# A state-space stage computed channels first, with its sum of squares made on TensorE

## The chip, the cores and the metric

The kernel runs on one core of a Trainium2 chip. The metric is the device time of one execution in microseconds. The kernel before has a median of 1835.91 us over three runs (1831.64 to 1842.42); the execution that was profiled took 1837.23 us, and the profile's span, from its first instruction to its last, is 1835.4 us. A measurement of this kernel tells a change of about 0.5% from none.

## The reference, cut to what matters

The program is two transformer-like layers. Its first part, the one that is changed, is a state-space mixer on 2 sequences of 512 tokens and 512 features, 64 heads of 64 channels in 8 groups of 8 heads:

```python
proj = hidden @ in_proj.T                    # gate 4096, x 4096, B 1024, C 1024, dt 64
xBC  = silu(conv_bias + causal 4-tap convolution of (x, B, C))
dt   = softplus(dt + dt_bias);  dA = exp(-dt * exp(A_log))
state = state * dA[t] + (dt[t] * x[t]) outer B[t]        # per head, 64 x 128
y[t]  = state @ C[t] + D * x[t]
yn    = y * rsqrt(mean(y*y over the group's 512 channels) + 1e-5) * norm_weight
out  += (yn * silu(gate)) @ out_proj.T
```

Behind it come a gated feed-forward layer with ternary weights, attention with 32 heads of 16 channels, and a layer of 8 experts of which each token takes 2, with norms and residual sums between them. They are the same in both kernels.

## The kernel before, in words

Every engine has a program of its own, written out by hand, and the engines meet only in semaphores; the order of each queue is the order of the code. The state-space stage is `step(g, s, first, last)` in each of the four engines' blocks. `group_steps` calls it for group 0 unrolled, groups 1 to 6 in a hardware loop, and group 7 unrolled with two more steps to drain. A step `s` is one tile of 128 tokens (`NT` = 8 tiles, `CH` = 4 per sequence), and it is a software pipeline: tile `s` is transposed and its decay matrices are made, tile `s-1` gets its outputs `y`, tile `s-2` is normalised and multiplied with the output projection. Steps 0, 1, 2, 4, 5 and 6 also make two of the 12 convolution tiles (6 per sequence, 128 channels by 512 tokens) for later steps; steps 3 and 7 make none (`conv_tiles`). In group 7 the steps from 4 on make none.

Products that need more than one pass are split in a high and a low half in `fp32r` (`products`, L344: 12 products of 128 by 128 by 512 for each 512 x 512 result tile). `low` (L349) makes the low half by a subtraction. Other products are plain fp32, and each of them is two records on TensorE.

In one step of the kernel before:

- TensorE: four transposes of `xbc` into bank 4 (L1482), B's transpose and the product of B and C (L1486, L1488), the sums of decays from `am` (L1496), the first convolution tile, four transposes of `yn` of tile `s-2` into bank 4 (L1515), `yo` = C times the state in bank 6 (L1523, 128x512, only where a state has entered, that is in 6 of 8 steps), `yi` in bank 7 as eight products, one for each head, `em` stationary and 64 columns of `dtx` moving (L1529), the new state's product in bank 6 (L1538, waits until VectorE has read `yo`), the second convolution tile, the gate product of tile `s` in bank 0, and the output product of tile `s-2` in bank 1. Tokens are on the partitions in `yo`, `yi`, `y`, gate and `yn`.
- VectorE: `btok` and `gmask` (L1170, L1173), `em` times `gmask` (L1176, waits for ScalarE's exponential), `y` = bank 6 times the growth `cur` (L1186), the three taps of the first convolution (L1100), `ynTl` (L349), `y` plus bank 7 (L1199), `y` plus `xd` (L1202; L1206 where no state entered), the state (L1212, L1215), `silu` (L1106), the second tile's taps, the gate `sg` (L1225), `yn` = `y` times `rg` times `sg` (L1233), `silu`, and the accumulation in `acc` (L1240). In step 3 it also subtracts two of the next group's `wcl`. In group 7 `norm_round` for the next layer follows L1240.
- ScalarE: the copy of `xtok` out of bank 4 (L881), the exponential `em` (L889), the first tap and the tanh of each convolution tile (L856, L864), `ynTh` out of bank 4 (L900), the square of `y` with its sum in `ss` (L907), the gate's tanh (L913). In step 3 it casts the next group's `wch`, at the end of step 7 the gate's (`gate_high`, L923) and scales the output weights (L926), in step 2 it casts those.
- GpSimd: the decays `am` of the next tile (L640, two of 128x1024), the state's decay (L667), `dtx`, `xdec` and `xd` = D times x (L677, L682, L686), the root `rg` (L691, L694), the low halves `wol` in step 2, `wcl` (two) in step 3 and `wgl` in step 7.
- SP: for each group the loads of `w_conv` (once `wgl` and `wol` are done), then `w_gate` and `w_out` (once `wcl` is done), all into the buffer `x`: gates in rows 0 to 3, outputs in 4 to 7.

Before the loop the first sequence's six convolution tiles of group 0 are made, with ScalarE and VectorE finishing each one before bank 0 or 2 is free again. In group 7 SP reloads the residual `hidden` into `x`.

Of the kernel before, what the change touches and what calls it, by code (L numbers as in the profile page):

```python
# [14 lines left out]
P = 128  # L15
# [42 lines left out]
def program(nc, hidden, w_conv, w_gate, w_dt, conv_w, conv_b, dt_bias, A_log, Dskip, norm_w, w_out,  # L58
            ff_gu, ff_dn, gate_s, up_s, down_s, wq, wk, bqk, wv, bv, wo, bo, gate_w, expert_w, out):
    ctx = ExitStack()  # L60
    with ctx:
# [55 lines left out]
        per = sa("per", [P, 5 * NT + 1, H])  # L117
        cur = sa("cur", [P, 5 * NT + 1, HG])
# [14 lines left out]
        xd = sa("xd", [P, GI])  # L133
        bcast = xd[:, 0:2 * H].rearrange("p (a h) -> p a h", a=2)
        state = sa("state", [P, GI])
        y = sa("y", [P, GI])
        ss = sa("ss", [P, 2])
        ssv = sa("ssv", [P, 2])
        rg = sa("rg", [P, 2])
        yn = sa("yn", [P, GI])  # L140
        sg = sa("sg", [P, 2, GI])
        ynTh = sa("ynTh", [P, GI], F32R)
        ynTl = sa("ynTl", [P, GI], F32R)
# [129 lines left out]
        am_ready, xd_ready, xdec_ready, dtx_ready, sdec_ready = (sem(s) for s in ("am_ready", "xd_ready", "xdec_ready", "dtx_ready", "sdec_ready"))  # L273
        m_ready, yo_ready, yo_used, yi_ready, y_part, y_ready = (sem(s) for s in ("m_ready", "yo_ready", "yo_used", "yi_ready", "y_part", "y_ready"))
        st_ready, state_ready, ss_ready, ssv_ready, rg_ready = (sem(s) for s in ("st_ready", "state_ready", "ss_ready", "ssv_ready", "rg_ready"))
        gate_ready, tg_ready, gate_used, yn_ready, yn_tr, o_ready, out_added = (sem(s) for s in ("gate_ready", "tg_ready", "gate_used", "yn_ready", "yn_tr", "o_ready", "out_added"))
# [58 lines left out]
        gate_stage, out_stage = x[:, 0:KT, :], x[:, KT:2 * KT, :]  # L335
# [31 lines left out]
        CONV_BANKS = (0, 2)  # L367

# [71 lines left out]
        def _(sp):  # L440
# [5 lines left out]
            sp.dma_start(per[:, 5 * NT, :], Dskip.partition_broadcast(P)).then_inc(small_in, 16)  # L446
# [6 lines left out]
            sp.dma_start(gate_stage, w_gate[0]).then_inc(wg_in, 16)  # L453
            sp.dma_start(out_stage, w_out[0]).then_inc(wo_in, 16)
            with sp.Fori(0, G - 1) as g:

                sp.wait_ge(wg_lo, KT * g + KT)
                sp.wait_ge(wo_lo, KT * g + KT)
                sp.dma_start(conv_stage(1), w_conv[bass.ds(g + 1, 1)]).then_inc(wc_in, 16)

                sp.wait_ge(wc_lo, 2 * g + KT + 2)
                sp.wait_ge(wc_lo2, 2 * g + KT + 2)
                sp.dma_start(gate_stage, w_gate[bass.ds(g + 1, 1)]).then_inc(wg_in, 16)
                sp.dma_start(out_stage, w_out[bass.ds(g + 1, 1)]).then_inc(wo_in, 16)
            sp.wait_ge(wg_lo, KT * G)
            sp.wait_ge(wo_lo, KT * G)
            for i in range(NT):
                sp.dma_start(x[:, i, :], hidden[i * P:(i + 1) * P, :]).then_inc(x_in, 16)
# [153 lines left out]
        def _(pool):  # L622
# [28 lines left out]
            def step(g, s, first, last):  # L651
                if s < NT and not (last and s == NT - 1):
# [11 lines left out]
                if s >= 1 and 1 <= c < CH - 1:  # L664

                    pool.wait_ge(yo_ready, entered(g, i) + c)
                    pool.tensor_tensor(pair(state[:, :]), pair(state[:, :]), heads(4 * NT + i),  # L667
# [3 lines left out]
                if s < NT:  # L671

                    pool.wait_ge(x_out, NT * g + s + 1)
                    src = pair(xtok[:, s % 2, :])
                    if not (first and s == 0):
                        pool.wait_ge(yi_ready, NT * g + s)
                    pool.tensor_tensor(pair(dtx[:, :]), src, heads(NT + s), ALU.mult).then_inc(dtx_ready, 1)  # L677
                    if s % CH < CH - 1:
# [3 lines left out]
                        pool.tensor_tensor(pair(xdec[:, :]), src, heads(3 * NT + s), ALU.mult).then_inc(xdec_ready, 1)  # L682
                if s < NT:
                    if not (first and s == 0):
                        pool.wait_ge(y_ready, NT * g + s)
                    pool.tensor_tensor(pair(xd[:, :]), src, heads(5 * NT), ALU.mult).then_inc(xd_ready, 1)  # L686
                if not (first and s == 0) and s <= NT:

                    n = NT * g + s
                    pool.wait_ge(ss_ready, n)  # L690
# [10 lines left out]
                if s == NT - 1 and not last:  # L701
                    gate_low(g + 1)
# [1163 lines left out]
```

## Time and profile before

| | |
|---|---|
| median of three runs | 1835.91 us |
| the profiled execution | 1837.23 us, span 1835.4 us |
| TensorE, products | 1620.2 us busy, 88% of the span |
| VectorE | 1297.8 us, 71% |
| GpSimd | 1006.7 us, 55% |
| ScalarE | 755.8 us, 41% |
| granted TensorE clock, mean | 0.940 of full |
| chain that ended last | TensorE 66%, VectorE 13%, GpSimd 7% |
| `yi` products (L1529) | 1024 records, mean 272 ns, 121.3 us |
| DMA | 79.7 MB, 43 GB/s |

A busy share is the time in which an engine worked on an instruction, over the whole span. Records of TensorE overlap: one that lasts 0.39 us can be followed by the next after 0.23 us, so starts are compared with starts. In the profile's rows PE is TensorE's products, PEld its weight loads, DVE VectorE, ACT ScalarE, POOL GpSimd. PEclk is the granted clock, 1.00 for 2.4 GHz and 0.50 for 1.2 GHz.

### The profile page before, as it was taken

The numbers are of one execution on the slowest core, as the hardware profiler recorded it, in microseconds if no ns is written. First come the engines' busy times: TensorE is split into PE (matmuls) and PEld (weight loads), VectorE is DVE, ScalarE is ACT, GpSimd is POOL, SyncE is SP. The second block draws the span as 40 slices with busy tenths as digits, with TensorE's granted clock in tenths as the row PEclk, the third lists the DMA queues.
The fourth block names the chain that finished last, engine by engine and source line by source line (L and its number), as shares of the span: only waits on it lengthen the run. The fifth ranks groups of instructions, "written<-read, shape, count | busy, mean of one in ns | idle before, by whom it ended". The sixth has DMA issues, their size and how long they took to land.

```text
span 1835.4 us, 25172 instructions
## 1 busy us (share of the span) xinstructions
PE 1620.2 (88%) x8696; PEld 1272.0 (69%) x8696; DVE 1297.8 (71%) x2037; ACT 755.8 (41%) x1389; POOL 1006.7 (55%) x861
## 2 busy tenths in 40 slices
PE   3699989999999999999999877997489999988692
PEld 2478768777877787778777656886356676767581
DVE  5687888787888778787778856555636776768525
ACT  2443433434434434434343213333136766664231
POOL 3376775776767767757766835003433443328554
PEclk9899999999999999999999978999589999998696
DMA  4001020020010010200201001212000000032344
GB/s 134 1 35 47 1 79 3 0 80 0 34 46 0 34 46 0 80 0 0 80 0 43 38 1 64 69 69 92 0 0 13 1 13 1 1 147 83 100 142 160
DMA packets 23303, 79.73 MB, mean 43 GB/s; under 512 B 6464, under 2 KB 6592, under 8 KB 17984
## 3 DMA queue, kind: packets, MB, share of 16 engines
q1 hardware_dynamic: 19552, 66.73, 10.1%
q0 software_dynamic: 3680, 12.06, 2.0%
q8 instruction: 43, 0.70, 0.2%
q14 instruction: 28, 0.23, 0.0%
HBM read 68.56 MB, written 10.22 MB: 43 GB/s over the span
## 4 chain that ended last, share of the span: by engine, by line
PE 66%; DVE 13%; POOL 7%; issue 6%; ACT 4%; DMA 3%; SPq 1%; POOLq 0%; DVEq 0%; ACTq 0%
PE banks L344 35%; PE banks L1597 6%; PE banks L1529 3%; PE banks L1716 3%; PE banks L1607 2%; PE banks L1538 2%; PE banks L1496 2%; DMA x<-in_w_conv 2%; PE banks L1675 2%; POOL wol L349 2%; PE banks L1706 2%; DVE acc L558 2%; POOL am L640 1%; DVE nmax L1322 1%; DVE tap L1100 1%
## 5 line engine op out<-in xcount | busy, mean ns | idle before, releaser
L640 POOL TENSOR_TENSOR am<-ah,upto 128x1024 fp32r<-128x1024 f32 x64 | 129.3, 2021 | 217.9 <-PE banks L1496 203.6
L1100 DVE SCALAR_TENSOR_TENSOR tap<-banks,parg,tap 128x511 f32<-128x511 f32 (+2 forms) x288 | 214.9, 746 | 30.3 <-ACT tap L856 23.5
L1176 DVE TENSOR_TENSOR em<-em,gmask 128x1024 f32<-128x1024 f32 x64 | 129.3, 2020 | 91.4 <-ACT em L889 90.9
L791 POOL TENSOR_SCALAR kz<-kst,head 128x512 fp32r<-128x512 f32 x64 | 99.1, 1568 | 160.0 <-DVE kst L1306 160.0
L344 PE MATMUL banks<-xTh,wch 128*128 128x512 f32 x384 | 166.4, 433 | 3.7 <-POOL wcl L349 2.4
L640 POOL TENSOR_TENSOR am<-al,upto 128x1024 fp32r<-128x1024 f32 x64 | 160.7, 2511 | 0.0
L344 PE MATMUL banks<-xTh,wcl 128*128 128x512 f32 x384 | 151.7, 395 | 0.0
L344 PE MATMUL banks<-xTl,wch 128*128 128x512 f32 x384 | 151.4, 394 | 0.0
L1032 ACT ACTIVATE prob<-banks,nmax 128x128 f32<-128x128 f32 (+3 forms) x256 | 121.8, 530 | 54.5 <-DVE nmax L1322 54.3
L1529 PEld LDWEIGHTS banks<-dtx,em 128*128 128x128 f32 x1024 | 123.2, 192 | 23.0 <-issue 21.3
L1322 DVE TENSOR_REDUCE nmax<-banks 128x2 f32<-128x256 f32 (+3 forms) x128 | 104.7, 818 | 40.4 <-PE banks L1707 40.3
L856 ACT ACTIVATE tap<-banks,parg 128x512 f32<-128x512 f32 x96 | 74.7, 778 | 139.7 <-PE banks L344 132.0
L864 ACT ACTIVATE th<-tap 128x512 f32<-128x512 f32 x96 | 60.5, 630 | 149.0 <-DVE tap L1100 146.1
L1529 PE MATMUL banks<-dtx,em 128*128 128x64 f32 x1024 | 121.3, 272 | 0.0
L344 PE MATMUL banks<-wgh,xTh 128*128 128x512 f32 x256 | 116.4, 455 | 0.8 <-DVE tap L1100 0.8
L344 PE MATMUL banks<-woh,ynTh 128*128 128x512 f32 x256 | 103.4, 404 | 5.8 <-DVE ynTl L349 5.8
L344 PE MATMUL banks<-wgl,xTh 128*128 128x512 f32 x256 | 105.5, 412 | 0.0
L1716 PE MATMUL banks<-ident,prob 128*128 128x128 f32 x640 | 95.6, 276 | 10.7 <-DVE pB L1332 7.2
L344 PE MATMUL banks<-wgh,xTl 128*128 128x512 f32 x256 | 105.0, 410 | 0.0
L344 PE MATMUL banks<-wol,ynTh 128*128 128x512 f32 x256 | 103.0, 402 | 0.0
L344 PE MATMUL banks<-woh,ynTl 128*128 128x512 f32 x256 | 102.6, 401 | 0.0
L349 POOL TENSOR_TENSOR awl<-prob,awh 128x512 fp32r<-128x512 f32 x8 | 10.1, 1298 | 160.5 <-ACT awh L988 131.5
(289 smaller groups left out, 4471.3 us busy)
## 6 DMA issues: line engine op xcount, KB each, us to landing
x<-in_w_conv SPq DMA_DIRECT2D x7, 1536.0 KB, 6.6
x<-in_w_gate SPq DMA_DIRECT2D x8, 1024.0 KB, 4.8
x<-in_w_out SPq DMA_DIRECT2D x8, 1024.0 KB, 6.8
eraw<-in_expert_w SPq DMA_DIRECT2D x8, 1024.0 KB, 7.2
gur<-in_ff_gu SPq DMA_DIRECT2D x7, 1024.0 KB, 4.8
x<-in_hidden SPq DMA_DIRECT2D x16, 256.0 KB, 4.3
mates<-yd SPq DMA_DIRECT2D x8, 512.0 KB, 4.3
dnr<-in_ff_dn SPq DMA_DIRECT2D x7, 512.0 KB, 3.5
```

The lines of the kernel that those rows point to most:

```text
L344: m = nc.tensor.matmul(o, a, b, start=first and n == 0, stop=last and n == len(terms) - 1)
L640: m = pool.tensor_tensor(am[:, part, :, :], a[:, i, :].bitcast(F32).unsqueeze(2).to_broadcast([P, HG, P]), upto[:, :].unsqueeze(1).to_broa ...
L791: m = pool.tensor_scalar(kz[:, quad % 2, p2, j, :], kst[:, p2, :].bitcast(F32), head[:, j:j + 1], None, ALU.mult)
L856: nc.scalar.activation(tap[:, q % 2, :], bk(CONV_BANKS[q % 2]), ACT.Identity, bias=parg[:, CT * KC + q:CT * KC + q + 1], scale=parg[:, KC ...
L864: nc.scalar.activation(th[:, :], tap[:, q % 2, :], ACT.Tanh).then_inc(tanh_ready, 1)
L1032: e = nc.scalar.activation(prob[:, n % 2, j, 0:kw], bk(2 * (n % 2) + j)[:, 0:kw], ACT.Exp, bias=nmax[:, n % 2, j:j + 1])
L1100: nc.vector.scalar_tensor_tensor(tap[:, q % 2, sh:L], bk(CONV_BANKS[q % 2])[:, 0:L - sh], parg[:, KC * q + k:KC * q + k + 1], tap[:, q % 2 ...
L1176: nc.vector.tensor_tensor(em[:, s % 2, :, :], em[:, s % 2, :, :], gmask[:, :].unsqueeze(1).to_broadcast([P, HG, P]), ALU.mult).then_inc(m_ ...
L1322: nc.vector.tensor_reduce(nmax[:, n % 2, :], banks[:, 2 * (n % 2):2 * (n % 2) + 2, 0:kw], AX, ALU.max, negate=True).then_inc(max_ready, 1)
L1529: m = mat(bk(7)[:, h * HP:(h + 1) * HP], em[:, i % 2, h, :], dtx[:, h * HP:(h + 1) * HP], start=True, stop=True)
L1597: m = mat(bk(2 * w + ft), gu[:, k, ft, w, :], part[:, k, tok], start=(k == 0 and part is xTh), stop=(k == KT - 1 and part is xTl))
L1716: m = pe.transpose(bk(4 + j)[:, c * P:(c + 1) * P], prob[:, w % 2, j, c * P:(c + 1) * P], ident[:, :])
```

## The change

The stage is turned: `y`, `yn` and the gate have channels on the partitions and tokens in the free dimension, so that `yn` needs no transpose before the output product.

- `yi`: `dtx` (64 columns) is stationary, `em` (128 columns) moves; the even heads' outputs go to partitions 0 to 63, the odd ones' to 64 to 127. `yo`: four products with 128 columns of the state stationary and C moving.
- The growth factors now run along the free dimension. They are made once for all heads, stored in DRAM (`grownT`), and for each tile where a state has entered SP loads them broadcast, by two DMAs into the single buffer `grown`, a row of `x`.
- `D * x` is no longer a GpSimd product: `skipped` adds it with four `scalar_tensor_tensor` on 128 columns each, reading `xbc`.
- The norm's factor is now a per-partition scalar only after the output product, so `rg` moves into the accumulation in `acc`. `y` is multiplied with the gate in place. The sum of squares: ScalarE squares `y` into `ysq`, four products of `ysq` with a column of ones add it up in bank 4, ScalarE scales it and adds eps (`ssv`), GpSimd takes the root.
- The four transposes of `yn` and `xd` go. `ynTh` and `ynTl` read `y` in SBUF.
- The gate is made in tiles of 128 channels by 512 tokens, three before the loop and one in each step; the last group has none in steps 5 to 7. The casts and low halves of the gate's weights move from step 7 to step 5, the load of `w_out` behind them.
- VectorE does `ynTl` ahead of the `em` multiply, and in steps without convolution tiles the entered part of `y` too.

```diff
-                    for j in range(KT):
-                        m = pe.transpose(bk(4)[:, j * P:(j + 1) * P], yn[:, j * P:(j + 1) * P], ident[:, :])
-                    m.then_inc(yn_tr, 1)
+                    for j in range(KT):
+                        m = mat(bk(4)[:, 0:1], ysq[:, j, :], ones[:, 0:1], start=(j == 0), stop=(j == KT - 1))
+                    m.then_inc(ss_ps, 1)
...
-                        mat(bk(6), xbc[:, JC, tok], state[:, :], start=True, stop=True).then_inc(yo_ready, 1)
+                        for j in range(KT):
+                            m = mat(bk(6)[:, j * P:(j + 1) * P], state[:, j * P:(j + 1) * P], xbc[:, JC, tok], start=True, stop=True)
+                        m.then_inc(yo_ready, 1)
...
                     for h in range(HG):
-                        m = mat(bk(7)[:, h * HP:(h + 1) * HP], em[:, i % 2, h, :], dtx[:, h * HP:(h + 1) * HP],
-                                start=True, stop=True)
+                        m = mat(bk(7)[h % 2 * HP:h % 2 * HP + HP, h // 2 * P:(h // 2 + 1) * P], dtx[:, h * HP:(h + 1) * HP],
+                                em[:, i % 2, h, :], start=True, stop=True)
...
+                def entered_part():
+                    at_least(dve, ynT_lo, NT * g + i)
+                    if c > 0:
+                        dve.wait_ge(yo_ready, m + c)
+                        dve.wait_ge(grown_in, 32 * (m + c))
+                        nc.vector.tensor_tensor(y[:, :, :], kt(bk(6)), grown, ALU.mult).then_inc(yo_used, 1)
+
+                def skipped(base):
+                    for k in range(KT):
+                        n = nc.vector.scalar_tensor_tensor(y[:, k, :], xbc[:, k, i % NT * P:(i % NT + 1) * P], skipg[:, k:k + 1],
+                                                           base[:, k, :], ALU.mult, ALU.add)
+                    n.then_inc(y_ready, 1)
...
+                if not (first and s < 2):
+                    dve.wait_ge(ynT_hi, NT * g + s - 1)
+                    low(nc.vector, ynTl[:, :, :], y[:, :, :], ynTh[:, :, :]).then_inc(ynT_lo, 1)
+                if s < NT:
+                    if s > 0 and not tiles:
+                        entered_part()
                     dve.wait_ge(e_ready, NT * g + s + 1)
...
+                if making:
+                    dve.wait_ge(sq_ready, NT * g + i + 1)
+                    dve.wait_ge(gate_used, NT * g + 4 + KT * (i // CH) if i >= 0 else NT * g)
+                    nc.vector.tensor_tensor(y[:, :, :], y[:, :, :], gate_at(i % NT), ALU.mult).then_inc(yn_ready, 1)
...
-                    nc.vector.tensor_tensor(acc[:, i % NT, :], acc[:, i % NT, :], bk(1), ALU.add).then_inc(out_added, 1)
+                    dve.wait_ge(rg_ready, NT * g + i + 1)
+                    nc.vector.scalar_tensor_tensor(acc[:, i % NT, :], bk(1), rg[:, i % 2:i % 2 + 1], acc[:, i % NT, :],
+                                                   ALU.mult, ALU.add).then_inc(out_added, 1)
...
+            def grown_load(g, i):
+                at_least(sp, yo_used, entered(g, i) + i % CH - 1)
+                for u in range(2):
+                    sp.dma_start(grown[HP * u:HP * u + HP, :, :],
+                                 halves[u][bass.ds(g, 1), :, i * P:(i + 1) * P].rearrange("g k t -> (g k) t").partition_broadcast(HP)
+                                 ).then_inc(grown_in, 16)
```

## Rows read from the trace of the kernel before

**Rows 1.** Stretches: the first and the last of the seven groups, busy by engine, clock

```profile
core 0: us, PE busy (x) PEld busy (x) DVE busy (x) ACT busy (x) POOL busy (x), PEclk, DMA share, GB/s
81.30:201.40 120.10, 114.94 (x558) 92.18 (x559) 96.28 (x129) 51.31 (x87) 87.99 (x68) 0.97 0.09 31
...
832.40:958.60 126.20, 122.71 (x609) 98.76 (x608) 99.64 (x139) 52.49 (x89) 87.64 (x69) 0.97 0.08 29
```

**Rows 2.** Stretches: steps 0, 2, 3 and 7 of group 3, and its sum

```profile
454.80:470.70 15.90, 15.90 (x83) 13.05 (x82) 13.33 (x21) 8.59 (x15) 13.04 (x10) 1.00 0.00 0
...
486.60:503.40 16.80, 16.80 (x84) 13.46 (x83) 12.92 (x17) 7.58 (x13) 14.82 (x11) 1.00 0.23 83
503.40:519.00 15.60, 12.97 (x60) 10.14 (x59) 12.85 (x17) 6.86 (x11) 13.34 (x10) 0.89 0.03 12
...
567.60:579.90 12.30, 11.44 (x60) 9.00 (x59) 9.24 (x14) 5.34 (x10) 10.16 (x9) 1.00 0.00 0
sum 125.10, PE 121.61 PEld 98.22 DVE 100.10 ACT 52.41 POOL 87.65; mean PE 15.20 PEld 12.28 DVE 12.51 ACT 6.55 POOL 10.96
```

**Rows 3.** Waits of TensorE over the whole span: total us, times, longest

```profile
PE banks L1538 <- DVE y L1186: 32.6, 18, 5.5
...
PE banks L1482 <- DVE xbc L1106: 6.8, 1, 6.8
```

**Rows 4.** Timeline of step 3 of group 3: start, us, engine, line

```profile
505.13 0.60 PE L1515 MATMUL banks<-ident,yn 128*128 128x128 f32 x4
505.56 1.02 PE L1523 MATMUL banks<-state,xbc 128*128 128x512 f32 x2
...
505.91 0.28 DVE L1170 COPY btok<-banks 128x128 f32<-128x128 f32 x1
...
506.42 1.89 PE L1529 MATMUL banks<-dtx,em 128*128 128x64 f32 x16
...
507.52 2.68 DVE L1176 TENSOR_TENSOR em<-em,gmask 128x1024 f32<-128x1024 f32 x1 [1.13 <-ACT em L889]
...
510.95 1.10 PE L1538 MATMUL banks<-xdec,btok 128*128 128x512 f32 x2 [2.63 <-DVE y L1186]
...
512.87 1.04 POOL L686 TENSOR_TENSOR xd<-xtok,cur 128x512 f32<-128x512 f32 x1 [0.77 <-DVE y L1202]
...
513.87 0.91 POOL L691 TENSOR_TENSOR ssv<-ss,epsc 128x1 f32<-128x1 f32 x1
...
515.98 3.69 POOL L349 TENSOR_TENSOR wcl<-x,wch 128x768 fp32r<-128x768 f32 x2
```

**Rows 5.** Timeline of TensorE at the router, products with few columns

```profile
1670.12 0.40 PE L344 MATMUL banks<-awl,attTh 128*128 128x512 f32 x1
1670.35 0.39 PE L344 MATMUL banks<-awh,attTl 128*128 128x512 f32 x1
1670.59 0.95 PE L1756 MATMUL banks<-rw,yb 128*128 128x8 f32 x8
1671.43 0.33 PE L1765 MATMUL banks<-ident,acc 128*128 128x128 f32 x1
```

**Rows 6.** Attention, products on 32-column tiles: timeline, then its weight loads (min/median/max ns)

```profile
1444.25 0.82 PE L1716 MATMUL banks<-ident,prob 128*128 128x128 f32 x6
1445.01 0.86 PE L1675 MATMUL banks<-pA,v 128*32 128x256 f32 x16
1445.79 0.50 PE L344 MATMUL banks<-xTh,aqh 128*128 128x512 f32 x1
...
L1675 PEld LDWEIGHTS banks<-pA,v x16: 106/110/110, 1445.0 to 1445.5; 128*32 128x32 f32 x16
```

**Rows 7.** Lines L1186 and L1202 on VectorE: min/median/max ns, first and last start

```profile
L1186 DVE TENSOR_TENSOR y<-banks,cur x48: 675/679/694, 114.9 to 1083.3; 128x512 f32<-128x512 f32 x48
...
L1202 DVE TENSOR_TENSOR y<-y,xd x48: 691/948/4382, 119.1 to 1085.3; 128x512 f32<-128x512 f32 x48
```

**Rows 8.** DMA issues: a load broadcast to all partitions, KB, us to landing

```profile
dsb<-in_down_s SPq DMA_DIRECT2D x1, 256.0 KB, 3.4
```

**Rows 9.** Stretch: step 6 of the last group

```profile
1046.50:1065.60 19.10, 13.59 (x60) 10.28 (x59) 13.93 (x20) 3.41 (x6) 13.63 (x15) 0.82 0.00 0
```

More of the change, by code:

```diff
@@ L651, in step @@
             def step(g, s, first, last):
+                if s == 5 and not last:
+                    gate_low(g + 1)
                 if s < NT and not (last and s == NT - 1):
@@ L868, in step @@
                 tiles = conv_tiles(s, last)
+                gate = gate_of(s, last)
+                i = s - 2
                 if s == 4 and tiles:
@@ L941, in _ @@
             tanh(0, 0)
-            for n, row in enumerate((2, 3, 4)):
+            for n, row in enumerate((2, 3)):
                 act.wait_ge(dt_cum, n + 1)
@@ L1150, in _ @@
                 silu(q, q, 0)
+                if q >= 3:
+                    gate_made(q - 2, (1, 7)[(q - 3) % 2], 0, q - 3)
             dve.wait_ge(consts, 7)
@@ L1155, in step @@
                 tiles = conv_tiles(s, last)
+                gate = gate_of(s, last)
+                i, c = s - 1, (s - 1) % CH
+                m = entered(g, i)
+                making = not (first and s == 0) and s <= NT
+                def entered_part():
[9 more added lines that the diff above has]
+                    n.then_inc(y_ready, 1)
                 if s == 4 and not last:
@@ L1472, in step @@
                 tiles = conv_tiles(s, last)
+                gate = gate_of(s, last)
                 if s < NT:
@@ L1541, in step @@
                     convolved(n0 + tiles[1], tiles[1] % CT, tiles[1] // CT % NB)
-                if s < NT:
-                    if s == 0:
-                        pe.wait_ge(wg_lo, KT * g + KT)
+                if gate:
+                    if s == 5:
+                        pe.wait_ge(wg_lo, KT * g + 2 * KT)
                     if tiles:
                         pe.wait_ge(taps, 3 * (n0 + tiles[0]) + 3)
-                    elif not (first and s == 0):
-                        pe.wait_ge(gate_used, NT * g + s)
-                    tok = slice(s * P, (s + 1) * P)
-                    products(bk(0), [(xTh[:, k, tok], xTl[:, k, tok], wgh[:, k, :], wgl[:, k, :])
-                                     for k in range(KT)]).then_inc(gate_ready, 1)
+                    else:
+                        pe.wait_ge(gate_used, NT * g + s + 3)
+                    gated(*gate, 0)
                 i = s - 2
```

252 lines of the change are left out of this document (153 added, 99 removed).

## The prediction, made before the changed kernel was run

> **What bounds the kernel now.** I read the page's busy shares first (they stand in the table above). They are means over four stages, so next come the stretches by head group [rows 1]. Seven groups of the state-space stage take 81.3 to 958.6 us, 48% of the span, and the eighth follows. Then one group by its eight steps [rows 2]: TensorE busy 121.6 of 125.1 us, VectorE 100.1. Where a step has convolution tiles, TensorE is busy for all of it (15.90 of 15.90, 16.80 of 16.80): only its own work counts there. Step 3 has no tiles and no such cover: 15.6 us, busy 12.97, granted clock 0.89. Step 7 loses about 1 us. The list of waits says which [rows 3]: the state product (L1538) waited 32.6 us for `y` (L1186). The timeline of step 3 [rows 4] shows it: the products with `em` end near 508.2, the state product starts at 510.95, and a part of the step behind this pause runs at the lower of the clock's two levels, which is how its mean comes to 0.89. L1186 waits because VectorE takes the `em` multiply first (507.52, 2.68 us).
>
> What should a whole group cost TensorE? Step 3's own work is a 16.8 us step without two tiles of 12 products, 0.233 us apart (two of this kind start at 1670.12 and 1670.35 [rows 5]), 11.2 us; likewise step 7. So 4 x 15.9 + 2 x 16.8 + 2 x 11.2 = 119.6 us. Seven groups would be 837.2, less 5.6 in group 0, whose first two steps have no output product: 831.6. They take 877.3 (81.3 to 958.6) [rows 1]. **45.7 us are stall or low clock**; the rest is bound by content.
>
> **Part 1, TensorE's content.** All of it is on the path in a full step.
> - Out: four transposes of `yn`, 0.43 us (505.13 to 505.56 [rows 4]). In: four fp32 products of `ysq` with one column. An fp32 product is two records, as L1523 x2 shows. The nearest row is the router's fp32 product with an 8-column moving side and a 128-column load: eight records in 0.84 us, 1670.59 to 1671.43 [rows 5]; fewer columns can't make it cheaper, as a record there advances at 0.108 us while 8 columns stream for almost nothing, so the load is the price. Bounds 0.43 to 0.95, taken 0.84: **+0.41**.
> - `yo`: one product of 512 columns (0.86 us, 505.56 to 506.42 [rows 4]) becomes four of 128, eight records at 0.11: **+0.03**, in 6 of 8 steps.
> - `yi`: now 16 records of 128-column loads and 64 columns; a record alone lasts 0.27 (table), so (1.89 - 0.27)/15 = 0.108 us each, 1.73 us together [rows 4]. The load sets that pace. Turned, loads are 64 columns and 128 columns stream, and the products alternate between the two column halves of the array. Twice the columns in the same number of records: everything hangs on the halves running together. The nearest row is the attention's product with `v` [rows 6]: 16 records on 32-column tiles, eight of 256 and eight of 128 columns, take 0.78 us to the next line; in a row they would be 8 x 0.21 + 8 x 0.108 = 2.6 us. So four tiles do overlap, loads included. Its edges cost: six transposes from 1444.25 on, 0.11 apart, so the last starts at 1444.80, and the first tiled record at 1445.01, 0.21 where 0.11 is usual, and on leaving the same, 0.1 each way. So 8 x 0.108 + 0.2 = 1.06 us: **-0.67**. Bounds: 0.86 (no edges) to 1.93 (halves in turn).
>
> Sum: -0.26 a step, +0.03 in six of eight: in 56 steps -14.6 + 1.3 = **-13.3 us**.
>
> **Part 2, the wait of step 3 and 7.** Steps without tiles now do `ynTl` and then `y` = `bk(6)` x `grown` ahead of the `em` multiply. In step 3 `yo` is through 1.9 + 0.84 + 0.89 = 3.6 us after its start, `y` at 4.4 to 4.6, and TensorE is ready for the state product at 4.7. The wait goes, and with it the low clock behind it. What is late next: the weights of the next group. TensorE reaches them 11.2 + 1.5 = 12.7 us after the step's start; GpSimd's last `wcl` ends at 516.0 + 3.7 = 519.7 now [rows 4], 16.3 after. It loses `xd` (1.04), the wait for `y_ready` ahead of it (0.77) and `ssv` (0.91); that puts it at 13.6, some 1 us late. VectorE and GpSimd then subtract at once and stretch each other, so I leave 1.5 us a group. Recovered: 45.7 - 7 x 1.5 = **-35.2 us**.
>
> **Part 3, VectorE, ScalarE, GpSimd.** `y + xd` becomes four instructions on 128 columns: `btok` on 128 columns takes 0.28 [rows 4], so 1.1 us for the 0.69 of one L1202 (bounds 0.7 and, should two SBUF inputs meet GpSimd as L1202's do at the median, 1.5). `ynTl` moves ahead of `em`, into time in which VectorE waits for the exponential; it now reads SBUF twice. The rows show what that means: the L1186 with one PSUM input never passes 0.694 us, L1202 with two SBUF inputs has median 0.948 and maximum 4.38 [rows 7]. VectorE is busy 12.5 us of a mean 15.6 [rows 2], so +0.4 us lies under TensorE: counted zero; without that cover it is 64 x 0.4 = 26 us. The square loses its accumulator read and gains a 128x1 activation; GpSimd is relieved. The gate casts and lows move from step 7 to step 5, in front of `em` and the decays: four casts put the exponential some 2 us later, and four subtractions of 1.3 us end near 7.5 us of the step, while the product that needs them starts near 10 (behind both convolution tiles). Hidden.
>
> **Part 4, DMAs.** 96 loads of 128 KB, two for each of six `grown`, one buffer. The nearest is a 256 KB broadcast, 3.4 us to landing [rows 8]. From one `y` to the next lie 10 us or more, so it is hidden, also on SP's queue: the load for step 4 stands behind `w_conv`, the loads for 7 and 0 behind `w_out`, each with a step to spare. If not hidden: up to 3.4 us in 48 steps.
>
> **Part 5, both ends.** Three gate products move ahead of the loop. There VectorE sets the pace and TensorE's first transposes (L1482) wait 6.8 us for its last one [rows 3]; but the last convolution now stands behind two gates (2 x 2.8), which wait for `wgl`. Estimated **+5.7** (3 to 9). In the last group steps 5 to 7 have no gate. Step 6 (19.1 us) runs at a mean clock of 0.82 [rows 9] and is a chain through `y`, state product, gate product, `sg` and output; the twelve gate products fall out of it, between 2.8 us at full clock and 5.6 at half, and `y` no longer stands behind `em` (2 us): -4.4; step 7 -3.7; steps 3, 8 and 9 about -1.3, -1.3 and -0.9; steps 0 to 2, 4 and 5 -1.5 together: **-13** (5 to 18).
>
> **Sum.** -13.3 - 35.2 - 13 + 5.7 = -55.8. The profiled execution took 1837.2 (span 1835.4 and 1.8 around it), 0.1% over the median 1835.9: **1781.5 us**, some 3%.
>
> **Rivals.**
> - *The stall stays.* `grown` or the weights arrive late in step 3 (DMA, or GpSimd and VectorE stretching one another). For: [rows 7], and only one `grown` buffer. Against: 10 us from one use to the next. -35 falls away: 1817.
> - *The halves run in turn*, loads hidden: `yi` 1.93 us. Against: [rows 6]. 64 x 0.87 more: 1837, no change.
> - *Slower: the halves run in turn and each load stands open.* Load records of 32 columns last 0.11 us [rows 6]; 16 x (0.108 + 0.11) + 0.2 = 3.7 us for `yi`, 64 x 2.6 more: 1951. It decides from `yi` above 1.93. Against it speak [rows 6]: there 16 loads and 16 products share 0.78 us. The Trainium skill ("TensorE: Matmul & The Clock Gate", Part 3, Packing small matmuls) says that a weight load overlaps matmuls in flight only where the row group differs; here all products use all rows, and by that rule this rival would be the outcome. The trace does not agree: in [rows 6], with all rows in use too, the loads are hidden.
> - *The change does nothing for TensorE's order*: excluded, 13 us are content.
>
> The skill's "TensorEngine Tiling (Array Packing)", Key Properties, has the array drain when the tiling mode changes; [rows 6] agree, with 0.1 us at each edge.
>
> **Numbers.** Forecast 0.75, its own range 1755 to 1808: `yi` 0.86 to 1.3 (-13, +15), 0 to 3 us left in a group (-10, +10), the ends (-8, +11), not all at once. Stall stays 0.13; in turn 0.07; slower 0.05. A measurement tells about 0.5% (9 us) from no change: faster 0.88, same 0.07, slower 0.05. The range reaches to the stalled case: 1755 to 1820.
>
> **What would show it.** Right: `yi`, 16 records with 128x128 moving, about 1.1 us to the next line; the `ysq` records 0.84; loop groups of 119 to 120 us; step 3 at 11 to 13 us with clock 1.00 and nothing waited for on `y` by the state product. Wrong: `yi` of 1.7 us or more; a wait of `y` on the `grown` DMA; VectorE busy through whole steps with TensorE waiting for taps or `gate_used`; loop groups still near 125.

## The result and the profile after

The changed kernel takes **1841.05 us** (median of 20 runs, 1839.62 to 1843.11) against 1834.72 us (20 runs, 1831.29 to 1844.32) of the kernel before: a ratio of **1.0033**, 95% interval 1.0023 to 1.0043. By the bound of 0.5% that is no change, though the interval puts it some 0.3% on the slow side; it is 59.6 us above the forecast. The profiled span is 1839.2 us where it was 1835.4.

The page shows TensorE a little less busy than before, VectorE 78 us busier, GpSimd 69 us less busy, and VectorE's share of the chain up from 13% to 21%:

```profile
PE 1605.8 (87%) x9254; PEld 1270.5 (69%) x9254; DVE 1375.8 (75%) x2223; ACT 759.5 (41%) x1390; POOL 938.1 (51%) x733
...
PE 67%; DVE 21%; issue 5%; ACT 3%; POOL 3%; DMA 1%; SPq 0%; DVEq 0%; POOLq 0%; ACTq 0%
...
x<-grownT SPq DMA_DIRECT2D x96, 128.0 KB, 4.8
```

The stretches show where. These are steps 0 to 4 and 7 of group 3 and their sum of eight, then the last of the seven groups and the sum of seven (us, then busy by engine, granted clock, DMA share, GB/s); they answer to [rows 1, 2]:

```profile
468.50:484.25 15.75, 15.75 (x92) 13.15 (x91) 14.09 (x23) 8.36 (x14) 6.93 (x5) 1.00 0.07 17
484.25:499.83 15.58, 15.58 (x86) 12.69 (x85) 15.31 (x23) 6.22 (x10) 7.31 (x5) 1.00 0.00 0
499.83:517.00 17.17, 16.63 (x95) 13.59 (x93) 14.96 (x19) 7.58 (x13) 14.38 (x10) 1.00 0.31 93
517.00:529.70 12.70, 11.60 (x70) 9.07 (x69) 12.37 (x18) 6.75 (x11) 10.40 (x7) 1.00 0.19 40
529.70:551.73 22.03, 17.58 (x92) 14.32 (x91) 18.22 (x26) 6.23 (x10) 9.80 (x6) 0.92 0.19 60
...
583.98:595.10 11.12, 11.11 (x70) 9.08 (x69) 9.38 (x16) 3.50 (x7) 7.72 (x5) 1.00 0.10 24
sum 126.60, PE 120.48 PEld 98.19 DVE 110.85 ACT 52.87 POOL 78.92; mean PE 15.06 PEld 12.27 DVE 13.86 ACT 6.61 POOL 9.87
...
847.93:974.25 126.32, 120.22 (x678) 97.96 (x677) 110.88 (x162) 52.88 (x89) 78.89 (x52) 0.99 0.13 42
sum 881.97, PE 837.14 PEld 680.89 DVE 766.51 ACT 367.94 POOL 551.03; mean PE 119.59 PEld 97.27 DVE 109.50 ACT 52.56 POOL 78.72
```

Step 3 fell from 15.60 to 12.70 us and its clock rose from 0.89 to 1.00; step 7 fell from 12.30 to 11.12; steps 0 and 1, 15.9 us each before, lost 0.15 and 0.3. But **step 4, 15.9 us before, now takes 22.03**, at a mean clock of 0.92. The group is 1.5 us longer instead of 6.9 shorter.

TensorE's waits over the whole span (total us, times, longest) name a new first term of this stage, once in each of the seven groups:

```profile
PE banks L350 <- DVE sg L1238: 31.1, 7, 4.5
PE banks L1651 <- DVE y L1264: 20.3, 18, 4.0
...
PE banks L350 <- POOL wgl L355: 4.7, 1, 4.7
```

L350 is the convolution product, L1238 `gate_made`, which frees the bank that the convolution writes; L1651 is the state product (L1538 before). The timeline of steps 3 and 4 (start, us, engine, line), first VectorE, then GpSimd, then TensorE:

```profile
520.96 1.33 DVE L355 TENSOR_TENSOR ynTl<-y,ynTh 128x512 fp32r<-128x512 f32 x1
...
523.03 2.10 DVE L1299 TENSOR_TENSOR em<-em,gmask 128x1024 f32<-128x1024 f32 x1
...
525.76 1.99 DVE L1269 SCALAR_TENSOR_TENSOR y<-xbc,skipg,y 128x128 f32<-128x128 f32 x4
527.68 0.68 DVE L1322 TENSOR_TENSOR state<-banks,state 128x512 f32<-128x512 f32 x1
528.28 4.56 DVE L355 TENSOR_TENSOR wcl<-x,wch 128x768 fp32r<-128x768 f32 x2
532.77 2.38 DVE L1335 TENSOR_TENSOR y<-y,sg 128x512 f32<-128x512 f32 x1
535.27 0.69 DVE L1238 SCALAR_TENSOR_TENSOR sg<-x,banks 128x512 f32<-128x512 f32 x1
...
527.61 4.42 POOL L355 TENSOR_TENSOR wcl<-x,wch 128x768 fp32r<-128x768 f32 x2
531.99 2.61 POOL L700 TENSOR_TENSOR am<-ah,upto 128x1024 fp32r<-128x1024 f32 x1
...
530.39 1.18 PE L1609 MATMUL banks<-am,after 128*128 128x512 f32 x4
536.02 0.80 PE L350 MATMUL banks<-xTh,wch 128*128 128x512 f32 x1 [4.45 <-DVE sg L1238]
536.61 0.63 PE L350 MATMUL banks<-xTl,wch 128*128 128x512 f32 x1
537.04 0.63 PE L350 MATMUL banks<-xTh,wcl 128*128 128x512 f32 x1
```

VectorE has no pause in the part shown from 523.03 on. It reaches the gate tile 18.3 us after the step's start; TensorE was ready for the convolution at about 531.57, 14.6 us after it. From 528.3 on both engines subtract at once. After 4.45 us of waiting, TensorE's first products start 0.43 us apart instead of 0.23: the granted clock is 0.50 from 536.02 to 539.2, the lower level again, paid on top.

Here is VectorE in the same step of the kernel before, which started at 503.40:

```profile
513.31 2.29 DVE L349 TENSOR_TENSOR wcl<-x,wch 128x768 fp32r<-128x768 f32 x2
...
517.11 0.69 DVE L1225 SCALAR_TENSOR_TENSOR sg<-sg,banks 128x512 f32<-128x512 f32 x1 [1.51 <-ACT sg L913]
517.72 2.50 DVE L1233 SCALAR_TENSOR_TENSOR yn<-y,rg,sg 128x512 f32<-128x512 f32 x1
```

There VectorE's two subtractions were over at 515.60, before GpSimd's began at 515.98 [rows 4]: the two did not meet. The change puts VectorE's at 11.3 us of the step instead of 9.9, and GpSimd's at 10.6 instead of 12.6, so now they do: 4.56 us instead of 2.29 on VectorE, 4.42 instead of 3.69 on GpSimd. The product with the gate was stretched before too (2.50 us, now 2.38; alone it takes 0.68), but it stood behind the gate tile. In the changed kernel it stands ahead of it (L1335, L1238), so its length counts now. The gate tile is through 19.0 us after the step's start, where it was through after 14.4.

### The profile page after: what moved, and what is told of

Same layout as the page of the kernel before. It is cut to its first block, busy times and chain, and to the rows that moved or that the text cites. A ratio compares the mean times of both kernels' runs of the same rounds, so it can differ in the third digit from the quotient of the medians.

```text
span 1839.2 us, 27053 instructions
## 1 busy us (share of the span) xinstructions
PE 1605.8 (87%) x9254; PEld 1270.5 (69%) x9254; DVE 1375.8 (75%) x2223; ACT 759.5 (41%) x1390; POOL 938.1 (51%) x733
## 4 chain that ended last, share of the span: by engine, by line
PE 67%; DVE 21%; issue 5%; ACT 3%; POOL 3%; DMA 1%; SPq 0%; DVEq 0%; POOLq 0%; ACTq 0%
PE banks L350 36%; PE banks L1718 6%; PE banks L1837 3%; PE banks L1728 2%; PE banks L1642 2%; PE banks L1796 2%; PE banks L1609 2%; PE banks L1626 2%; DVE y L1269 2%; PE banks L1651 2%; PE banks L1827 2%; PE banks L1635 2%; DVE wcl L355 2%; DVE acc L618 2%; DVE tap L1184 1%
## 5 line engine op out<-in xcount | busy, mean ns | idle before, releaser
L700 POOL TENSOR_TENSOR am<-ah,upto 128x1024 fp32r<-128x1024 f32 x64 | 136.6, 2134 | 257.8 <-PE banks L1609 243.5
L1184 DVE SCALAR_TENSOR_TENSOR tap<-banks,parg,tap 128x511 f32<-128x511 f32 (+2 forms) x288 | 214.9, 746 | 25.7 <-ACT tap L911 18.9
L350 PE MATMUL banks<-xTh,wch 128*128 128x512 f32 x384 | 170.7, 444 | 31.1 <-DVE sg L1238 31.1
L1299 DVE TENSOR_TENSOR em<-em,gmask 128x1024 f32<-128x1024 f32 x64 | 142.9, 2233 | 26.0 <-ACT em L963 25.8
L350 PE MATMUL banks<-xTh,wcl 128*128 128x512 f32 x384 | 155.0, 404 | 0.0
L350 PE MATMUL banks<-xTl,wch 128*128 128x512 f32 x384 | 154.6, 403 | 0.0
L700 POOL TENSOR_TENSOR am<-al,upto 128x1024 fp32r<-128x1024 f32 x64 | 148.6, 2322 | 0.0
L350 PEld LDWEIGHTS banks<-xTh,wch 128*128 128x128 f32 x384 | 75.5, 197 | 59.2 <-DVE sg L1238 29.7
L350 PE MATMUL banks<-xTh,wgh 128*128 128x512 f32 x256 | 108.5, 424 | 5.2 <-POOL wgl L355 4.7
L350 PE MATMUL banks<-woh,ynTh 128*128 128x512 f32 x256 | 103.3, 404 | 8.1 <-DVE ynTl L355 8.1
L739 POOL TENSOR_TENSOR dtx<-xtok,cur 128x512 f32<-128x512 f32 x64 | 75.0, 1172 | 61.1 <-PE banks L1642 60.9
L350 PE MATMUL banks<-woh,ynTl 128*128 128x512 f32 x256 | 101.8, 398 | 0.0
L350 PE MATMUL banks<-xTh,wgl 128*128 128x512 f32 x256 | 101.8, 398 | 0.0
L350 PE MATMUL banks<-wol,ynTh 128*128 128x512 f32 x256 | 101.5, 396 | 0.0
L350 PE MATMUL banks<-xTl,wgh 128*128 128x512 f32 x256 | 101.3, 396 | 0.0
L983 ACT ACTIVATE ysq<-y 128x512 f32<-128x512 f32 x64 | 40.3, 630 | 136.6 <-DVE y L1269 135.9
```

The source lines that it names most:

```text
L350: m = nc.tensor.matmul(o, a, b, start=first and n == 0, stop=last and n == len(terms) - 1)
L700: m = pool.tensor_tensor(am[:, part, :, :], a[:, i, :].bitcast(F32).unsqueeze(2).to_broadcast([P, HG, P]), upto[:, :].unsqueeze(1).to_broa ...
L739: pool.tensor_tensor(pair(dtx[:, :]), tokens, heads(s), ALU.mult).then_inc(dtx_ready, 1)
L1184: nc.vector.scalar_tensor_tensor(tap[:, q % 2, sh:L], bk(CONV_BANKS[q % 2])[:, 0:L - sh], parg[:, KC * q + k:KC * q + k + 1], tap[:, q % 2 ...
L1299: nc.vector.tensor_tensor(em[:, s % 2, :, :], em[:, s % 2, :, :], gmask[:, :].unsqueeze(1).to_broadcast([P, HG, P]), ALU.mult).then_inc(m_ ...
```

## The experiments

The theory: step 3 now puts VectorE's whole queue on the path. That queue holds `ynTl`, four skip products (`skipped`), the state, two `wcl` subtractions beside GpSimd's two, the product of `y` with the gate, and the gate tile. The rivals: one piece of that queue alone (the skip products), the plain order in it, or the place of the convolution in TensorE's queue. Where a version leaves work out, its output is not the program's; it serves only to time the rest.

**The convolution later in step 4.** The first convolution tile moves behind the squares' sum, `yo` and `yi`. Only TensorE's order (and ScalarE's wait for new parameters) changes:

```diff
-                if tiles:
-                    if s == 4:
-                        pe.wait_ge(wc_lo, 2 * g + KT + 2)
-                        pe.wait_ge(wc_lo2, 2 * g + KT + 2)
+                if tiles and s != 4:
...
+                if tiles and s == 4:
+                    pe.wait_ge(wc_lo, 2 * g + KT + 2)
+                    pe.wait_ge(wc_lo2, 2 * g + KT + 2)
```

> The changed kernel with one order moved: in step 4 TensorE makes the first convolution tile behind the squares, yo and yi instead of ahead of them, and ScalarE waits for the new taps only ahead of the first tap. If VectorE's queue of step 3 is what step 4 waits for, TensorE now has 2.9 us of other work first: the wait of 4.5 us shrinks to about 1.5, the low clock behind it goes, step 4 falls from 22.0 to about 17 us, seven groups by 33 us, the whole to about 1808 us. If the wait is for something that comes later still (GpSimd's low halves), step 4 stays at 20 us or more and the whole above 1825.

Measured: 1820.36 us, ratio to the kernel before 0.9929 (0.9906 to 0.9953), where about 1808 was expected. Step 4 of group 3 among the stretches:

```profile
517.73:536.91 19.18, 16.05 (x92) 13.13 (x91) 18.71 (x25) 6.22 (x10) 10.16 (x6) 1.00 0.20 68
```

And TensorE's waits:

```profile
PE banks L350 <- DVE sg L1238: 11.4, 7, 1.7
PE banks L350 <- DVE tap L1184: 11.2, 8, 1.6
```

The clock stays at 1.00 and step 4 gives back 2.9 of its 6.1 us, no more: VectorE is busy for 18.71 of 19.18 us. TensorE still waits 1.6 us for the gate tile in this step and then 1.5 for the taps, so a part of the lag is only moved. The order on TensorE is a part of the cost; what is late is VectorE.

**Without the skip products.**

```diff
-                    for k in range(KT):
-                        n = nc.vector.scalar_tensor_tensor(y[:, k, :], xbc[:, k, i % NT * P:(i % NT + 1) * P], skipg[:, k:k + 1],
-                                                           base[:, k, :], ALU.mult, ALU.add)
+                    if base is y:
+                        n = nc.vector.tensor_copy(y[:, 0, 0:1], y[:, 0, 0:1])
+                    else:
+                        n = nc.vector.tensor_copy(y[:, :, :], base)
```

> The changed kernel without D times x (the four small instructions of VectorE per step are left out; where no state has entered one copy stands for them). If these four are what delays VectorE in step 3 (the rival), step 4 falls back from 22.0 to 15.6 us and the whole to about 1796. If the whole queue of step 3 is too long, only their 1.9 us come off, step 4 falls to 19 to 20 us and the whole to 1820 to 1828. If GpSimd's low halves decide, nothing moves.

**Without the low halves of the convolution weights** (the subtractions cut to one column each, on GpSimd in the same way).

```diff
-                        low(nc.vector, wcl[:, k, :], conv_stage(1)[:, k, :], wch[:, k, :]).then_inc(wc_lo2, 1)
+                        low(nc.vector, wcl[:, k, 0:1], conv_stage(1)[:, k, 0:1], wch[:, k, 0:1]).then_inc(wc_lo2, 1)
```

> The changed kernel with the next group's low halves wcl cut to one column each on VectorE and GpSimd (the rest of the low half is left out). Queue theory: VectorE is through with the gate of step 3 some 5 us earlier, step 4 takes 15.6 us without a wait, a group 120 us, the whole about 1796. If another thing made TensorE wait in step 4 (the gate's own tanh, the taps), step 4 stays above 19 us.

Measured: 1796.84 us without the skip products, 1795.54 without the low halves (one run each). Each alone takes nearly all of the stall away. The first number is the one expected of the rival, that the skip products alone are the cause (about 1796); the queue theory had put it at 1820 to 1828 and missed it. But the second, with all skip products in place, is the one expected of the queue theory. Step 4 is 17.24 us in the first and 15.76 in the second, a group 121.6 and 120.4, the seven groups 842.7 and 837.2. So neither piece is the cause by itself: the stall needs both. The rows of `wcl` show why (min, median and max ns). First the changed kernel:

```profile
L355 POOL TENSOR_TENSOR wcl<-x,wch x14: 1869/2224/2580, 146.5 to 908.9; 128x768 fp32r<-128x768 f32 x14
L355 DVE TENSOR_TENSOR wcl<-x,wch x14: 2017/2315/2619, 147.2 to 909.6; 128x768 fp32r<-128x768 f32 x14
```

Then the kernel without the skip products:

```profile
L355 DVE TENSOR_TENSOR wcl<-x,wch x14: 946/1028/1178, 144.4 to 872.2; 128x768 fp32r<-128x768 f32 x14
L355 POOL TENSOR_TENSOR wcl<-x,wch x14: 2196/2250/2304, 145.9 to 874.8; 128x768 fp32r<-128x768 f32 x14
```

In its list of waits, what is left in step 4:

```profile
PE banks L350 <- POOL wcl L355: 9.3, 7, 1.8
```

Taking out the skip products, 1.99 us in step 3, saved 4.8 us of step 4, because VectorE's subtractions then run mostly before GpSimd's (in group 3 from 507.76 to 509.81, GpSimd's from 509.31) and cost 1.03 us each instead of 2.32. GpSimd's stay at 2.25: they now run beside the product with the gate, which takes 2.35. What remains is the kind of wait that the prediction had foreseen, for GpSimd's last `wcl`: 9.3 us in seven groups against 10.5. That the sizes agree is luck, since both ends of it come later than it had them: GpSimd is through at 15.5 us of the step, not 13.6.

**All low halves on VectorE.** This takes the meeting away and adds two instructions to the queue that is late.

```diff
-                if s == 3 and not last:
-                    for k in (2, 3):
-                        pool.wait_ge(wc_hi, KT * g + KT + k + 1)
-                        low(pool, wcl[:, k, :], conv_stage(1)[:, k, :], wch[:, k, :]).then_inc(wc_lo, 1)
...
-                    for k in (0, 1):
+                    for k in range(KT):
```

> The changed kernel with all four low halves wcl on VectorE, none on GpSimd. If GpSimd's late low halves are what step 4 waits for (as the prediction had it), its wait goes and the whole falls towards 1800. If VectorE's queue is, two more of 1.15 us stand in it, but none is stretched by GpSimd's: their sum stays near 4.6 us, the product with the gate behind them takes 0.7 instead of 2.4, step 4 falls by 1 to 2 us, the whole to about 1830.

Measured: 1809.69 us (one run), step 4 17.72 us. The row of `wcl`, alone on VectorE:

```profile
L355 DVE TENSOR_TENSOR wcl<-x,wch x28: 942/947/950, 145.3 to 881.6; 128x768 fp32r<-128x768 f32 x28
```

The timeline of VectorE in step 3:

```profile
512.04 3.55 DVE L355 TENSOR_TENSOR wcl<-x,wch 128x768 fp32r<-128x768 f32 x4
515.51 0.68 DVE L1331 TENSOR_TENSOR y<-y,sg 128x512 f32<-128x512 f32 x1
```

My number was too high by 20 us, since I had charged too little to the meeting. One engine does four subtractions in 3.55 us; two engines at once need 4.56 and 4.42 us for two each, and the product behind them takes 2.38 us instead of 0.68. The help of the second engine is worth less than nothing here.

**The gate ahead of VectorE's low halves**, a test of the plain order.

```diff
-                if s == 3 and not last:
-                    for k in (0, 1):
-                        dve.wait_ge(wc_hi, KT * g + KT + k + 1)
-                        low(nc.vector, wcl[:, k, :], conv_stage(1)[:, k, :], wch[:, k, :]).then_inc(wc_lo2, 1)
...
                     gate_made(NT * g + s + 4, 0, *gate)
+                if s == 3 and not last:
+                    for k in (0, 1):
+                        dve.wait_ge(wc_hi, KT * g + KT + k + 1)
+                        low(nc.vector, wcl[:, k, :], conv_stage(1)[:, k, :], wch[:, k, :]).then_inc(wc_lo2, 1)
```

> The changed kernel with VectorE's two low halves of the convolution weights in step 3 put behind the product of y with the gate and behind the gate tile, so that the gate bank is free first and the low halves are what the next convolution waits for. Theory A (both engines subtract at once and stretch each other; what is needed is the sum of the work and the overlap is the price): the product with the gate now meets GpSimd's two subtractions and is stretched to 1.5 to 2.4 us, VectorE's two low halves come last and still meet the end of GpSimd's, about 1.0 to 2.0 us each; TensorE's first convolution product starts 16.5 to 18.5 us after the start of step 3 instead of 19.0, step 4 is 19.5 to 21.5 us and the whole 1823 to 1837 us. Rival B (only the place of the gate in the queue counts, since it stood last): TensorE would be held no longer than GpSimd's own 15 us, step 4 about 18 us, the whole about 1813 us. Rival C (order does not matter at all): 22.0 us and 1841 us.

Measured: 1836.77 us (one run), step 4 21.39 us. The gate tile is no longer waited for; the low halves are. From the list of waits, then from the timeline:

```profile
PE banks L350 <- DVE wcl L355: 22.7, 6, 3.8
```

```profile
528.94 4.36 DVE L355 TENSOR_TENSOR wcl<-x,wch 128x768 fp32r<-128x768 f32 x2
...
529.88 2.60 POOL L700 TENSOR_TENSOR am<-ah,upto 128x1024 fp32r<-128x1024 f32 x1
```

Moved behind the gate, VectorE's subtractions are stretched nearly as much as before (4.36 us for 4.56); `am`, GpSimd's next work, now runs beside them. This order inside the queue gives 0.6 us of 6.1. Rival B (about 18 us and 1813) falls. Theory A (19.5 to 21.5 and 1823 to 1837) holds at its upper edge, and rival C, that order does not matter (22.0 and 1841), is missed by only 0.6 us a group. What the run shows is that the stretch does not go away by moving the subtractions. The other order, the gate tile ahead of the stretched product as in the kernel before, is not open to the changed kernel: in step 3 the new tile (`gate_kept(1, 2)`) is written over the one that the product reads (`gate_at(2)`).

**The kernel before, with only `y` moved ahead of `em` in steps 3 and 7.** No turning, no skip products.

```diff
+                        if not tiles:
+                            entered_part()
                     dve.wait_ge(e_ready, NT * g + s + 1)
...
+                if tiles or s >= NT:
+                    entered_part()
```

> The kernel before with one part of the change alone: in steps without convolution tiles VectorE multiplies bank 6 into y ahead of the em multiply. If a wait of TensorE in step 3 is only handed on (queue theory), step 3 falls from 15.6 to 11.5 to 12.5 us and step 4 grows from 15.9 to 18 or 19, since the low halves end 16.3 us after step 3's start and are needed after 12.7; step 7 falls by 1 us; the whole 1820 to 1830. If the wait simply goes, step 4 stays at 15.9 and the whole comes to about 1800.

Measured: 1829.15 us (one run), within the 1820 to 1830 expected, but by another sum: step 4 was expected at 18 or 19 us. Steps 3, 4 and 7 of group 3 and the sum:

```profile
505.20:516.44 11.24, 11.24 (x60) 8.93 (x59) 10.59 (x15) 6.86 (x11) 9.19 (x7) 1.00 0.04 17
516.44:538.87 22.43, 18.97 (x82) 15.05 (x81) 16.32 (x22) 6.01 (x10) 14.12 (x10) 0.85 0.24 94
...
571.53:582.78 11.25, 11.25 (x61) 8.93 (x60) 7.00 (x14) 5.36 (x10) 9.15 (x8) 1.00 0.00 0
sum 126.25, PE 122.79 PEld 98.98 DVE 101.60 ACT 52.53 POOL 88.57; mean PE 15.35 PEld 12.37 DVE 12.70 ACT 6.57 POOL 11.07
```

And TensorE's wait in step 4:

```profile
PE banks L344 <- POOL wcl L349: 24.1, 7, 3.5
```

This is the clearest reading of all. The seven groups take 878.5 us, 877.3 before. The order alone clears step 3 to 11.24 us, the 11.2 that the prediction had worked out for it, and step 4 takes it back and more: 15.9 to 22.4. The stall is handed on, to GpSimd's `wcl` here, to VectorE in the changed kernel. GpSimd's last `wcl` ends 16.5 us after the step's start, where it ended after 16.3 before: the wait for `y` had been cover for it. The rest of step 4's growth is the lower clock behind the 3.46 us of waiting (mean 0.85). What the whole gains is in the last group, which has no next weights: its steps 0 to 6 take 99.0 us, 107.0 before.

**All outputs of `yi` in one column half.**

```diff
-                        m = mat(bk(7)[h % 2 * HP:h % 2 * HP + HP, h // 2 * P:(h // 2 + 1) * P], dtx[:, h * HP:(h + 1) * HP],
+                        m = mat(bk(7)[0:HP, h // 2 * P:(h // 2 + 1) * P], dtx[:, h * HP:(h + 1) * HP],
```

> The changed kernel with all eight products of yi written to partitions 0 to 63 (the odd heads overwrite the even ones, the other half is left out), so that both halves of the array are not used in turn. If the halves run together in the changed kernel and loads are hidden in any case, yi takes 16 x 0.108 + 0.1 to 0.2 = 1.8 to 1.9 us instead of 1.02; 64 steps of 0.8 to 0.9 more, less what step 4 hides: about 1885 to 1895. If a load stood open in one half, yi would take 2.5 us or more and the whole over 1930.

Measured: 1881.5 us (one run), below the 1885 to 1895 expected; a full step is some 0.85 us longer. The timeline of step 0 of group 3 in the changed kernel, then in this one:

```profile
472.97 0.95 PE L1626 MATMUL banks<-ones,ysq 128*128 128x1 f32 x8
473.78 1.14 PE L1635 MATMUL banks<-xbc,state 128*128 128x128 f32 x8
474.85 1.09 PE L1642 MATMUL banks<-em,dtx 128*64 128x128 f32 x16
475.87 0.50 PE L350 MATMUL banks<-xTh,wch 128*128 128x512 f32 x1
```

```profile
490.10 1.96 PE L1642 MATMUL banks<-em,dtx 128*64 128x128 f32 x16
491.99 0.50 PE L350 MATMUL banks<-xTh,wch 128*128 128x512 f32 x1
```

From start to start `yi` takes 1.02 us against 1.89: the halves do run together, loads included. The starts of the single records say the same: in the changed kernel they come in eight pairs, 0.01 us apart or less and 0.11 from pair to pair, in the other one by one, 0.11 apart. (The run in one half also lets the odd heads' products write over the even ones'; no run keeps these two effects apart, but a pace of 0.11 is that of the full-width records too.)

**Two versions from what was learned.** The first has all low halves on VectorE, the first convolution tile of step 4 between `yo` and `yi`, and the three gate products before the loop behind the last convolution instead of among them. The second also lets ScalarE multiply `D * x` into `ysq`, so that VectorE adds it in one instruction:

```diff
+                    for k in range(KT):
+                        j = (s - 1) % NT
+                        n = nc.scalar.activation(ysq[:, k, :], xbc[:, k, j * P:(j + 1) * P], ACT.Copy, scale=skipg[:, k:k + 1])
+                    n.then_inc(skipped_in, 1)
...
-                    for k in range(KT):
-                        n = nc.vector.scalar_tensor_tensor(y[:, k, :], xbc[:, k, i % NT * P:(i % NT + 1) * P], skipg[:, k:k + 1],
-                                                           base[:, k, :], ALU.mult, ALU.add)
+                    dve.wait_ge(skipped_in, NT * g + i + 1)
+                    nc.vector.tensor_tensor(y[:, :, :], base[:, :, :], ysq[:, :, :], ALU.add).then_inc(y_ready, 1)
```

> The changed kernel with three orders moved: all four low halves wcl on VectorE (as in lows_on_dve), in step 4 the first convolution tile behind yo and ahead of yi (1.9 us of other work ahead of it, against the 1.75 us of wait that lows_on_dve has left), and the three gate products ahead of the loop behind the last convolution tile. Queue theory: step 4 takes 15.8 us, a group 120.4, seven groups 14 us less than in lows_on_dve (849.5), the loop starts at 84 us instead of 92; the whole about 1787 us. If TensorE then waits for the taps ahead of the gate product (as it does 1.6 us in conv_later), step 4 stays at 17 and the whole at 1797.

> As combined2, but D times x is made by ScalarE (four instructions with a scale per partition into ysq) and added by one instruction of VectorE on 512 columns, so that VectorE has 0.4 us less in each step. If VectorE still delays steps 2 and 3 (17.2 and 12.7 us, 1.6 above their own work), they fall by about 0.4 each and the whole is near 1783. If ScalarE's queue becomes what is waited for (1.1 us more per step ahead of the tanh), it is slower than combined2.

Measured: 1793.87 us, ratio 0.9773 (0.9729 to 0.9818), and **1780.67 us, ratio 0.9694 (0.9652 to 0.9735)**. The first lies between the two numbers expected (1787 and 1797), its step 4 at 16.55 us; the second comes out as expected (1783), though only steps 3 and 4 fell and step 2 stayed at 17.16. The second's steps 3 and 4, sum, and seven groups:

```profile
486.58:498.53 11.95, 11.12 (x71) 9.08 (x69) 11.66 (x16) 8.01 (x15) 9.01 (x5) 1.00 0.18 52
498.53:514.42 15.89, 15.89 (x93) 12.97 (x92) 15.43 (x23) 7.39 (x14) 6.31 (x5) 1.00 0.26 83
...
sum 119.67, PE 118.27 PEld 96.86 DVE 102.44 ACT 62.55 POOL 75.62; mean PE 14.78 PEld 12.11 DVE 12.80 ACT 7.82 POOL 9.45
...
sum 831.05, PE 819.81 PEld 669.68 DVE 709.34 ACT 436.08 POOL 528.45; mean PE 117.12 PEld 95.67 DVE 101.33 ACT 62.30 POOL 75.49
```

Step 4 is full and the group 119.7 us, of which TensorE is busy 118.3; two waits for `y`, 0.5 and 0.8 us, are left. This version beats both kernels. That it lands on the 1781.5 us forecast for the changed kernel is luck: it gets there with other orders and other waits. The loop starts at 85.6 us in the first version and at 92.3 in the changed kernel (91.7 to 94.1 in the other versions of it), so the gates' place ahead of the loop is worth 6 to 8 us of its gain.

## Why the prediction was wrong

The forecast was 55.8 us less than before, in span +3.8 was measured. The 59.6 us between lie in three places: the seven groups 53.2 (828.8 predicted, 882.0 measured), the part ahead of the loop 5.3, the end 1.2.

**Part 1, TensorE's content: right, but `yo` was taken too short.** `yi` takes 1.02 us (1.06 predicted), the squares' sum (L1626) 0.81 ahead of `yo` and 0.88 ahead of `yi` (0.84), by the timeline's starts. `yo` takes 1.07 where 0.89 was predicted. By the starts of its records, 0.08 of this lie behind its first record, and are there too where a convolution follows instead of `yi` (the first version above, 1.10 us); 0.10 are the edge into the column halves, which the prediction had entered inside `yi`. So the gain is 0.15 us in a step with `yo` instead of about 0.23, some 4 us over 42 steps. The two rivals on the halves were wrong, as the run in one half shows. The loads were hidden in one half too, so the rule on row groups of the Trainium skill ("TensorE: Matmul & The Clock Gate", Part 3, Packing small matmuls) fits neither run. The same section of the Trainium skill also lets a load into the background weight buffer go ahead of matmuls in flight; no run shows whether that hid them here.

**Part 2: here the prediction failed, in "What is late next" and its 1.5 us a group.** Its first half was mostly right: the state product's waits for `y` fell from 3.5 to 1.5 us a group (0.5 in step 2, 1.0 in step 3), and the low clock left step 3. But `y` came 6.1 us after the step's start, not 4.4 to 4.6, as VectorE reached `ynTl` late and took 1.33 us for it. The prediction then followed one chain to the next use, GpSimd's `wcl`, and put its end at 13.6 us of the step; it came at 15.0, which alone would have held TensorE for some 0.5 us. It did not follow VectorE's own queue to the gate tile, which the next convolution's bank needs, and that came at 19.0. The change had made this queue longer by some 2 us in the very step that has no tiles (four skip products of 1.99 us for one L1202 of 0.69, `ynTl` 1.33 for 0.68), and had put the gate tile behind the product with the gate (2.38). And I named the stretching in a sentence and priced it inside those 1.5 us, where it measured 1.4 us on each of VectorE's two subtractions and 0.35 on each of GpSimd's two. The list of what would show the prediction wrong did name this case (TensorE waiting for `gate_used`, loop groups near 125), but no term of the sum priced it.

With the low halves out, the seven groups take 837.2 us; so 44.8 of the 53.2 us go with them. The other 8.4 are what else came on top (18.9 in all: the state product's waits in that run's trace 11.7, the edge and `yo` some 4, the rest small pauses in step 3), less the 10.5 that the prediction had allowed for the weights.

That the stall is handed on and not removed needs nothing of the turning: the old kernel with the new order alone shows step 3 at 11.24 and step 4 at 22.43. The hint stood in [rows 4]: GpSimd's `wcl` ended at 519.67, and TensorE's first product with the new weights started at 520.72. The slack was 1.05 us; all that the stall gave back beyond it had to come out of the queues of GpSimd and VectorE.

**Part 3: "counted zero" holds only under cover, and I said so** ("without that cover it is 64 x 0.4"), but charged it nowhere, though step 3 has no cover. There the four skip products took 1.99 us and `ynTl` 1.33. In steps 0 and 1 VectorE, at 14.09 and 15.31 of 15.7 us busy, cost nothing, as predicted; step 2 loses 0.5 us to `y`, and does so without the skip products too (17.17 us in both). The gate's casts and lows in step 5 were hidden: its 15.60 us are all TensorE.

**Part 4: right.** 4.8 us to landing instead of 3.4, and no engine waited for `grown`.

**Part 5: the signs right, the front too small by half.** Ahead of the loop +11.0 us against 5.7 predicted, outside 3 to 9: the first gate waited 4.7 us for `wgl` and its products then ran at the lower clock, with the last convolution behind them. The end saved 11.8 against 13.

As a rival, "the stall stays" (1817 us) was the right family and too mild: it had both engines stretching each other, but let no step get longer than it had been, and 1841 is beyond it.

## What to carry over

When a stall goes, walk every engine's queue, not only the chain you see, from the step's start to the next thing that the freed engine needs, and compare the ends with its new, earlier arrival: a wait on the bottleneck is cover for all that runs beside it. Before you share work that reads SBUF twice between VectorE and GpSimd, try all of it on VectorE (here 3.55 us for what took both 4.4 to 4.6), and count a new instruction at full price in any step where the bottleneck has no filler. A small swap in a copy of the old kernel (here the order alone) shows cheaply whether a stall is removed or handed on.

## What was not expected of the hardware

- In this step VectorE and GpSimd slow each other by more than they gain. A subtraction of 128x768 with both inputs in SBUF takes VectorE 0.947 us alone (0.942 to 0.950, 28 of them) and 2.315 at the median beside GpSimd's (2.017 to 2.619); the 128x512 product with the gate takes 0.68 alone and 2.38 beside GpSimd's `am` (in the kernel before 2.50 beside GpSimd's subtractions). GpSimd's subtraction went from 1.87 to 2.22 at the median. It is not always VectorE that gives way: with all low halves on VectorE the product ran beside `am` in 0.68 us, and `am` took 2.52 instead of 1.90. No run shows what decides it. VectorE's instructions with one input in PSUM stayed at 0.68 to 0.69 (L1264, L1309).
- Products on one 64-column half are as fast as plain ones and two halves run side by side: 16 records with 128 moving columns in 1.02 us against 1.89 in one half, with the weight loads hidden in both, though all use the same rows.
- The edges of the halves cost 0.1 us each: from the last record of `yo` to the first of `yi` pass 0.21 us where 0.11 is usual, and as much on leaving `yi`. Another 0.08 us lie behind the first record of `yo`, whatever follows it; no run shows why.
